# Attention scores of a tile as one two-bank PSUM tensor: one maximum and one subtraction per tile

## The reference

```
q = (x @ Wq + bq)            # 512 rows a batch, 16 heads
k = (ctx @ Wk + bk)          # 64 context rows
v = (ctx @ Wv + bv)
scores = einsum(q, k) * 16 ** -0.5          # 16 heads x 64 values for each row
attn = softmax(scores, axis=-1)
out = einsum(attn, v)
layer 0:  x = x + tanh(g) * (relu(out @ W1 + b1) @ W2 + b2)
layer 1:  x = x + tanh(g) * (out @ Wo + bo)
```

## Time and profile before

| | |
|---|---|
| median of three runs | 624.98 us (622.17, 624.98, 625.14) |
| profiled execution | 620.89 us, span 619.1 us |
| attention of layer 0 | from about 20 to 199 us |
| router and experts | from about 199 to 434 us |
| attention of layer 1 | from about 434 to 536 us |
| feed-forward of layer 1 | from about 536 us to the end |
| DVE, all stages | busy 382.0 us in 782 instructions |
| TensorE clock, granted, mean | 0.904 |

### The profile page before, as it was taken

The page is one execution under the profiler, slowest core; times in us unless marked ns, Lnnn a source line. Parts: engine busy times, 40 slices in busy tenths (PEclk is TensorE's granted clock), DMA queues, the critical chain, the costliest instruction groups (busy, mean ns, idle before and its releaser), DMA issues.

```text
span 619.1 us, 10659 instructions
## 1 busy us (share of the span) xinstructions
PE 502.2 (81%) x3557; PEld 393.8 (64%) x3558; DVE 382.0 (62%) x782; ACT 259.9 (42%) x441; POOL 252.9 (41%) x322
## 2 busy tenths in 40 slices
PE   4767988888794399999999999939487877558994
PEld 2443846657684199999999999924355544335552
DVE  4387888797834644342424422225879998868993
ACT  1234746344460054342433332311354454526884
POOL 3364234254400252020101010037245868737996
PEclk9967989999596589999999999975689899697999
DMA  7930010000055134933465210013000000000101
GB/s 209 298 119 1 1 35 2 34 1 1 34 203 201 54 127 133 332 118 103 153 228 180 74 32 19 17 51 94 1 0 1 2 0 1 1 1 0 35 34 68
DMA packets 28631, 46.38 MB, mean 75 GB/s; under 512 B 2380, under 2 KB 24920, under 8 KB 26552
## 3 DMA queue, kind: packets, MB, share of 16 engines
q1 hardware_dynamic: 24328, 39.02, 18.8%
q0 software_dynamic: 1680, 4.59, 2.5%
q10 hardware_dynamic: 2592, 2.36, 1.1%
HBM read 38.36 MB, written 7.60 MB: 74 GB/s over the span
## 4 chain that ended last, share of the span: by engine, by line
PE 48%; DVE 30%; issue 7%; POOL 6%; ACT 4%; DMA 3%; ACTq 0%; DVEq 0%; SPq 0%; POOLq 0%
PE bank L917 20%; PE bank L929 7%; DVE s_max L1363 5%; DVE p_sum L1381 5%; DVE probs L1371 4%; PE bank L662 4%; PE bank L778 3%; PE bank L995 3%; DVE stats L1296 2%; DVE ew L1318 2%; DVE xn L1318 2%; ACT probs L1062 2%; DVE x_res L1510 1%; PE bank L632 1%; PE bank L633 1%
## 5 line engine op out<-in xcount | busy, mean ns | idle before, releaser
L917 PE MATMUL bank<-q_t,ew 128*128 128x128 f32 x1152 | 136.7, 277 | 1.4 <-DVE probs_t L1639 1.0
L917 PEld LDWEIGHTS bank<-q_t,ew 128*128 128x128 f32 x1152 | 132.8, 193 | 3.1 <-DVE probs_t L1639 2.0
L470 POOL TENSOR_TENSOR probs<-probs,p_rcp 128x1024 f32<-128x1024 f32 x32 | 61.0, 1908 | 109.7 <-DVE p_rcp L1384 109.7
L1639 DVE TENSOR_TENSOR probs_t<-bank,probs 128x512 f32<-128x512 f32 x36 | 24.8, 690 | 78.4 <-ACT probs L1184 78.4
L690 PE MATMUL bank<-ident,probs 128*128 128x128 f32 x256 | 41.4, 314 | 31.7 <-POOL probs L470 28.9
L690 PEld LDWEIGHTS bank<-ident,probs 128*128 128x128 f32 x256 | 33.8, 162 | 43.8 <-POOL probs L470 33.3
L529 POOL TENSOR_TENSOR token_now<-token_of,carried 128x1 uint32<-128x1 uint32 x17 | 4.9, 286 | 126.9 <-PE bank L903 126.8
L1062 ACT ACTIVATE probs<-probs 128x1024 f32<-128x1024 f32 x32 | 33.9, 1058 | 51.9 <-DVE probs L1371 51.9
L1092 ACT COPY probs_t<-bank 128x512 f32<-128x512 f32 x64 | 35.0, 588 | 45.1 <-PE bank L690 45.0
L1363 DVE TENSOR_REDUCE s_max<-bank 128x8 f32<-128x512 f32 x64 | 40.4, 672 | 15.4 <-PE bank L675 15.2
L1184 ACT ACTIVATE probs<-bank 128x512 f32<-128x512 f32 x36 | 21.5, 599 | 62.8 <-PE bank L917 62.8
(11 more groups left out here) (207 smaller groups left out, 1095.7 us busy)
## 6 DMA issues: line engine op xcount, KB each, us to landing
ew<-in_L_ffn_w SPq DMA_DIRECT2D x8, 2048.0 KB
ew<-in_L_ffn_w SPq DMA_DIRECT2D x8, 1024.0 KB, 5.9
slots_y<-xn ACTq DMA_DIRECT2D x18, 128.0 KB, 2.0
x_res<-in_x SPq DMA_DIRECT2D x4, 512.0 KB, 6.8
token_rows<-ew SPq DMA_DIRECT2D x4, 512.0 KB, 3.0
out_rows<-x_res SPq DMA_DIRECT2D x3, 512.0 KB, 2.9
w<-in_L_xattn_W SPq DMA_DIRECT2D x2, 512.0 KB, 8.6
ew<-in_L_ffn_w_gate SPq DMA_DIRECT2D x1, 1024.0 KB, 9.0
```

Of the source, the lines that this page charges most:

```text
L470: nc.gpsimd.tensor_tensor(p, p, p_rcp[:, i, :].unsqueeze(2).to_broadcast([P, H, M]), ALU.mult).then_inc(s["p_norm"], 1)
L917: last = nc.tensor.matmul(o[:, P * j:P * j + P], ew1[:, s, k, c0:c0 + P], xs_t[:, par, k, :], start=(k == 0), stop=(k == DK - 1))
```

## The change

The four banks of the scores become two PSUM tensors of 1024 values, `s_tile[0]` (banks 0 and 1) and `s_tile[1]` (banks 2 and 3). `s_bank[i][g]` is now a view of one half, so all matmuls write where they wrote before. DVE takes the maximum of all 16 heads with one instruction over the whole tensor and subtracts it with one, each reading across the border of two banks. Waits and semaphore counts are the same. Heads lie in `s_max` and `probs` in the order group, chunk, head, the order of the banks. Sum, reciprocal and normalisation go by head and do not care; the transposes on PE do, and take their blocks from other places of `probs`, so that `t_bank` and all behind it are as before.

```diff
-        bank = [ctx.enter_context(nc.psum_tensor(f"bank{i}", [P, 512], F32)) for i in range(8)]
-        s_bank = [bank[0:2], bank[2:4]]
+        s_tile = [ctx.enter_context(nc.psum_tensor(f"s_tile{i}", [P, G * 512], F32)) for i in range(2)]
+        s_bank = [[s_tile[i][:, 512 * g:512 * g + 512] for g in range(G)] for i in range(2)]
+        bank = [*s_bank[0], *s_bank[1],
+                *(ctx.enter_context(nc.psum_tensor(f"bank{i}", [P, 512], F32)) for i in range(4, 8))]
...
-                            last = nc.tensor.transpose(t_bank[c][:, P * j:P * j + P],
-                                                       probs[:, i % 2, P * (4 * c + j):P * (4 * c + j + 1)], ident[:])
+                            at = P * (j // 2 * 4 + 2 * c + j % 2)
+                            last = nc.tensor.transpose(t_bank[c][:, P * j:P * j + P], probs[:, i % 2, at:at + P], ident[:])
...
-                for r in range(G):
-                    last = nc.vector.tensor_reduce(group_heads(s_max[:, i, :], r),
-                                                   s_bank[i % 2][r][:].rearrange("p (m h s) -> p m h s", m=DK, h=GH),
-                                                   AX, ALU.max)
-                last.then_inc(s["v_max"], 1)
+                nc.vector.tensor_reduce(s_max[:, i, :], s_tile[i % 2][:].rearrange("p (h s) -> p h s", h=H), AX,
+                                        ALU.max).then_inc(s["v_max"], 1)
                 dve.wait_ge(s["v_max"], g + 1)
                 if i >= 2:
                     dve.wait_ge(s["t_pt"], 2 * g - 2)
-                for r in range(G):
-                    last = nc.vector.tensor_tensor(
-                        probs[:, i % 2, :].rearrange("p (m g h s) -> p g m h s", m=DK, g=G, h=GH)[:, r],
-                        s_bank[i % 2][r][:].rearrange("p (m h s) -> p m h s", m=DK, h=GH),
-                        group_heads(s_max[:, i, :], r).unsqueeze(3).to_broadcast([P, DK, GH, M]), ALU.subtract)
-                last.then_inc(s["v_sub"], 1)
+                nc.vector.tensor_tensor(probs[:, i % 2, :].rearrange("p (h s) -> p h s", h=H),
+                                        s_tile[i % 2][:].rearrange("p (h s) -> p h s", h=H),
+                                        s_max[:, i, :].unsqueeze(2).to_broadcast([P, H, M]),
+                                        ALU.subtract).then_inc(s["v_sub"], 1)
```

More of the change, by code:

```diff
@@ L1352, in spread_values @@
                         ALU.add).then_inc(v_vbd, 1)
-            def group_heads(per_head, r):
-                return per_head.rearrange("p (m g h) -> p g m h", m=DK, g=G)[:, r]
             def scores(l, n, i):
```

## The result

The changed kernel takes 620.35 us against 623.8 us for the kernel before, both the median of 22 runs; the ratio is 0.9944 with a 95% interval of 0.9924 to 0.9964. That is 3.5 us less, with an interval of 2.2 to 4.7 us; the forecast was 3.3 us less. The profiled execution took 621.87 us, not the 617.6 us of the prediction, and has a span of 620.1 us, a microsecond longer than that of before (619.1), so the two traces must be compared stage by stage and not by their ends.

A forecast was written before the change was run, and what follows sets the result against it. DVE was taken to bound layer 1, PE and DVE in turn layer 0; 27 tiles x 0.12 us = 3.3 us, so 625.0 - 3.3 = 621.7 us, range 617.5 to 625.0 us.

The forecast's parts named there:

- The price of an instruction: Maximum and subtraction on DVE: one instruction instead of a pair saves 0.06 us each, 0.12 us a tile.
- Layer 1: Attention stage of layer 1: DVE is the bound, some 15 tiles of 16 pay, stage shorter by about 1.8 us.
- Layer 0: Attention stage of layer 0: the chain alternates between PE and DVE, 12 tiles of 16 pay, stage shorter by 1.4 us.
- The first rival: Gain lost in layer 0 to PE, ACT or POOL; only layer 1's 15 tiles pay, 1.8 us, 623.2 us; chance 0.20.
- The sum: Whole kernel: 27 tiles x 0.12 us = 3.3 us less, 621.7 us against the median.
- The clock rival: A block of queries on PE changes clock, 2.3 us either way: 619.4 or 624.0 us; chance 0.12, half each side.
- The new hold: Layer 1 rows at 476.41 us, 0.25 us after POOL's `rstd`: 0.12 us earlier, they still miss it, so no hold.

The follow-up runs named there:

- the runs with four: Each step of a tile in four instructions of 256 values instead of two, against the kernel before: ratio 1.0122; in layer 0 alone 1.0063, layer 1 alone 1.0052.

## Why the prediction was right, and where not

**The price of an instruction** was right: 0.12 us a tile forecast, 0.125 measured on the busy times, 0.065 us for each further instruction in the runs with four. Reading the start times of two neighbours instead of their lengths made the difference between 0.12 and 0.30 us a tile. The wide instruction's lengths, 1.16 to 1.22 us and 1.22 us, agree with what the sum of the softmax had shown; nothing was paid for the border of two banks. The fixed 120 cycles that the Trainium skill gives for a VectorE instruction that reads PSUM ("VectorE: DVE Perf Modes", the section on the extra latency of SBUF-source operations) would have given an estimated 0.25 us a tile; the runs disagree with 0.125.

**Layer 1** was right: 15 tiles x 0.12 = 1.8 us, measured 1.71, which at 0.125 us is the worth of 14 tiles, and 4.0 for 3.9 with four instructions.

**Layer 0** was mis-sized: 1.4 us forecast, 0.9 measured. The step that failed is "following the waits place by place I find 12 tiles that pay there". Nine of them pay, 1.1 us, and the other three take 0.2 back. I asked at each place whether DVE was last, not what stands behind it. At the last tile ACT's copy of `up_t` was less than the tile's gain behind and took over. At tile 1 of the third and the fourth batch no engine took over: the gain reached PE's product, and DVE's own queue then started the residual sum 0.3 and 0.1 us late, which no row of before could show and whose cause is open. The first rival (layer 0 loses its gain) named PE, ACT or POOL and was right in that way at one place only.

**The sum** was 3.3 us; the two stages give 2.6 us in the traces and the medians 3.5 us with an interval of 2.2 to 4.7. Each agrees with the other within that interval. That the medians came within 0.2 us of the forecast while the stages fell 0.7 us short of it is in part luck. Whether something of the gain lies in how often PE's lower clock strikes can't be said from these runs.

**The clock rival** gave 2.3 us for a block of queries; the traces with 10.3 instead of 7.6 us a step show 2.7 us each, of which 1.4 and 2.0 reach the end of the stage. The four traces of before and of the changed kernel show no such step. In the trace with single instructions in layer 1 alone it covers the gain.

**The new hold** that was looked for at 476.41 us did not come; no step of layer 1 became longer.

## What to carry to other kernels

Price the removal of a DVE instruction by the distance of the starts of two neighbours, less the stream: here 0.065 us each, while its own row reads 0.68 us and suggests more than twice the gain. Count the tiles that pay by how far the next engine is behind, not by whose name stands in the chain of waits: the gain of 0.125 us a tile was enough to hand the chain to ACT at the last tile, and at two other places it came to PE and was lost behind it. The chain of waits alone misleads here: in the changed kernel it names ACT for the hidden units too, where the starts show that nothing was lost. And where a difference is smaller than what one block of matmuls at the lower clock costs, compare stages between marks in the traces, which repeated here within 0.1 us unless the clock fell, before believing a median.

## What was not expected

A slowdown and a speedup of the same steps are not passed on alike: in layer 0 the worth of 12 tiles one way, of 7 the other. The TENSOR_SCALARs of DVE on rows in SBUF are held while POOL's TENSOR_TENSOR runs (3.29 against 1.38 us for four), while a maximum and a subtraction that read PSUM are not: in the trace of before those at 102.22 and 103.47 us took their usual 1.22 and 1.29 us beside POOL's product from 102.38 to 104.29. And after such a hold was taken away, PE ran two blocks at a granted clock of 0.50 instead of 1.00: of the 2.0 us by which they started earlier, 1.7 were given back in the one trace.
